# A recurrence with a mixture of experts on one core: side pieces due one block later, history ring cleared before the routing, rank products per choice

## What is computed

```python
dt = soft_clamp(softplus(xn @ Wdt.T + bdt), 0.001, 0.1, 0.5)
dA = exp(soft_clamp(dt[..., None] * A, -8.0, 8.0, 0.5));  dB = dt * (xn @ WB.T)
def step(h, inp):                      # 1024 steps, in order
    h = dAt * h + dBt * xt[..., None]
    h_norm = sqrt(sum(h * h, axis=(1, 2)))
    h = h * minimum(20.0 / (h_norm + 1e-08), 1.0)
    y = einsum('bdn,bn->bd', h, Ct) + Dp * xt
```

## Time and profile before

| | |
|---|---|
| device time, median of 3 | 1767.44 us (1767.29 to 1767.97) |
| device time of the profiled execution | 1766.3 us |
| its span, first to last instruction | 1764.2 us |
| DVE busy | 1550.5 us (88%) |
| PE busy | 1302.9 us (74%), granted clock 0.862 |
| ACT busy | 1227.6 us (70%) |
| POOL busy | 770.1 us (44%) |

### The profile page before, as it was taken

How to read it: one execution, slowest core, us unless ns; L and a number is a source line. 1 busy time by engine, 2 the same in 40 slices (tenths; PEclk the granted TensorE clock), 3 DMA queues, 4 the chain that set the end, 5 groups by cost and what they waited for, 6 DMA issues and landing times.

```text
span 1764.2 us, 33864 instructions
## 1 busy us (share of the span) xinstructions
PE 1302.9 (74%) x9352; PEld 1143.0 (65%) x9352; DVE 1550.5 (88%) x9455; ACT 1227.6 (70%) x3152; POOL 770.1 (44%) x1254
## 2 busy tenths in 40 slices
PE   5674434389879797987979797987979697835661
PEld 5553433378768686876868686876868586734551
DVE  6588888888979998997989899998989799997778
ACT  4587547388687887868687877878787777746451
POOL 3146666533434343433434343343434344468842
PEclk8577767699999898988989899998999899967885
DMA  9921111200111020111102002011101110012245
GB/s 335 340 92 49 46 43 42 96 25 24 41 55 37 25 71 24 37 59 31 31 17 91 18 26 71 27 41 34 55 24 49 40 31 19 19 34 73 75 126 195
DMA packets 95533, 113.29 MB, mean 64 GB/s; under 512 B 8432, under 2 KB 85360, under 8 KB 95344
## 3 DMA queue, kind: packets, MB, share of 16 engines
q1 hardware_dynamic: 87696, 94.13, 16.6%
q0 software_dynamic: 6144, 16.79, 3.0%
q10 hardware_dynamic: 1504, 0.22, 0.1%
HBM read 60.91 MB, written 50.20 MB: 63 GB/s over the span
## 4 chain that ended last, share of the span: by engine, by line
DVE 47%; PE 23%; ACT 9%; issue 8%; POOL 8%; DMA 3%; POOLq 0%; SPq 0%; DVEq 0%; ACTq 0%
DVE arena L756 10%; DVE arena L733 8%; DVE arena L745 7%; DVE arena L741 7%; DVE arena L727 7%; DVE arena L760 4%; PE ps L1213 4%; PE ps L1197 4%; POOL arena L536 4%; ACT arena L875 4%; PE ps L1185 4%; POOL xg L515 3%; PE ps L1160 3%; PE ps L1179 2%; DVE arena L730 2%
## 5 line engine op out<-in xcount | busy, mean ns | idle before, releaser
L536 POOL TENSOR_TENSOR arena<-arena,neghalf 128x1 f32<-128x1 f32 x1025 | 591.7, 577 | 881.1 <-DVE arena L730 812.0
L756 DVE SCALAR_TENSOR_TENSOR arena<-arena 128x128 f32<-128x128 f32 x1024 | 362.6, 354 | 53.3 <-POOL arena L536 53.1
L1185 PE MATMUL ps<-arena,pick 128*128 128x128 f32 x2048 | 306.7, 298 | 39.5 <-ACT arena L971 20.1
L1185 PEld LDWEIGHTS ps<-arena,pick 128*128 128x128 f32 x2048 | 285.1, 214 | 51.3 <-ACT arena L971 38.2
L971 ACT ACTIVATE arena<-ps,arena 128x128 f32<-128x128 f32 x1024 | 292.2, 377 | 35.1 <-PE ps L1185 34.7
L1179 PE MATMUL ps<-ident,arena 128*128 128x128 f32 x1024 | 211.8, 335 | 136.9 <-ACT arena L875 132.0
L1197 PE MATMUL ps<-arena,wf 128*128 128x256 f32 x1280 | 302.8, 387 | 8.1 <-issue 8.1
L741 DVE CUSTOM_DVE_ANT_0 arena<-arena 128x128 f32<-128x128 f32 x1024 | 294.2, 287 | 10.1 <-PE ps L1144 7.7
L1213 PE MATMUL ps<-wp,arena 128*128 128x256 f32 x1280 | 296.2, 385 | 5.4 <-ACT arena L979 5.1
L733 DVE CUSTOM_DVE_ANT_0 arena<-arena 128x128 f32<-128x128 f32 x1024 | 299.1, 292 | 0.0
L727 DVE TENSOR_TENSOR arena<-arena 128x128 f32<-128x128 f32 x1024 | 289.9, 283 | 4.5 <-POOLq L531 4.5
(11 more groups left out here) (147 smaller groups left out, 1380.3 us busy)
## 6 DMA issues: line engine op xcount, KB each, us to landing
xg<-zeros SPq DMA_DIRECT2D x10, 1024.0 KB, 9.1
xrow<-xg SPq DMA_DIRECT2D x40, 256.0 KB, 2.8
yg<-arena SPq DMA_DIRECT2D x40, 256.0 KB, 2.2
arena<-in_x SPq DMA_DIRECT2D x16, 512.0 KB, 9.3
wf<-in_c_fc SPq DMA_DIRECT2D x8, 1024.0 KB, 5.0
wp<-in_c_proj SPq DMA_DIRECT2D x8, 1024.0 KB, 5.9
arena<-dx SPq DMA_DIRECT2D x66, 64.0 KB, 2.3
ys<-arena SPq DMA_DIRECT2D x66, 64.0 KB
```

Source lines behind the costliest of these rows:

```text
L536: g.tensor_tensor(sv[:, slot, 1:2], mx, neghalf[:, 0:1], ALU.pow).then_inc(s_ready, 1)
L756: v.scalar_tensor_tensor(hr[:, slot, :], vv, sv[:, before, 1:2], ur[:, slot, :], ALU.mult, ALU.add)\
L1185: last = t.matmul(ps[2][:, j * P:(j + 1) * P], pick[:, q * QUAD + j, :], xin, start=True, stop=True)
```

## The change

Four edits. (1) The windows of all three kinds of pieces move one block (16 steps) later. (2) The routing's tiles leave `hr`'s memory: the small ones go behind the windows, into the experts' buffers, and the four large ones into `wp`. With that POOL clears `hr` and the windows without waiting for `route_ready`. (3) As `wp` is in use until then, SP loads tiles 8 to 15 (home 1) after `route_ready`. (4) The copy into `ohb` is gone. PE forms the rank products for each choice on its own, two of 256 columns as soon as the choice's one-hot array is there, and two more for the second. A new semaphore `rt_out` takes over the last use of `rt_in`.

```diff
-        at2 = [hr_at]
+        at2 = [hr_at + RING * P + BLK * NG * WIN]
...
-        ohb = lay(NE * 2 * JT).rearrange("p (e k j) -> p e k j", e=NE, k=2)
-        ohf = lay(NE * 2 * JT).rearrange("p (e k j) -> p e k j", e=NE, k=2)
...
+        ohf = wp.rearrange("p k d -> p (k d)")[:, 0:512].rearrange("p (e k j) -> p e k j", e=NE, k=2)
...
-            for table, pieces, lo_, hi_ in ((sum_at, 1, 4 * h - 9, 4 * h - 7), (input_at, 2, 4 * h - 6, 4 * h - 4), (norm_at, 1, 4 * h - 3, 4 * h - 1)):
+            for table, pieces, lo_, hi_ in ((sum_at, 1, 4 * h - 8, 4 * h - 6), (input_at, 2, 4 * h - 5, 4 * h - 3), (norm_at, 1, 4 * h - 2, 4 * h)):
...
             load_rows(0)
-            load_rows(1)
             sp.wait_ge(route_ready, 1)
-            for n in range(2, 6):
+            for n in range(1, 6):
                 load_rows(n)
...
             g.memset(sv, 1.0).then_inc(init_win, 1)
-            pool.wait_ge(route_ready, 1)
             g.memset(hr, 0.0).then_inc(h_ready, 1)
             g.memset(win, 0.0).then_inc(init_win, 1)
...
-                hop(v.tensor_tensor(ohf[:, :, k, :], iom, eix[:, k, :].unsqueeze(1).broadcast_to([P, NE, JT]), ALU.is_equal))
+                v.tensor_tensor(ohf[:, :, k, :], iom, eix[:, k, :].unsqueeze(1).broadcast_to([P, NE, JT]), ALU.is_equal).then_inc(rt_in, 1)
                 if k == 0:
+                    dve.wait_ge(rt_in, 1)
                     hop(v.scalar_tensor_tensor(lgw, ohf[:, :, 0, :], -3e38, lg, ALU.mult, ALU.add))
             v.tensor_tensor(pw[:, 0, :], top[:, 1, :], top[:, 0, :], ALU.subtract).then_inc(gap_ready, 1)
-            v.tensor_copy(ohb, ohf).then_inc(rt_in, 1)
...
-            v.tensor_copy(slot_of[:, :, :], rank).then_inc(rt_in, 1)
+            v.tensor_copy(slot_of[:, :, :], rank).then_inc(rt_out, 1)
...
-            pe.wait_ge(rt_in, 1)
-            flat = ohb.rearrange("p e k j -> p (e k j)")
-            t.matmul(ps[7][:, :], lows, flat, start=True, stop=True)
-            t.matmul(ps[6][:, :], ones[:, :], flat, start=True, stop=True).then_inc(rank_ps, 1)
+            for k in range(2):
+                pe.wait_ge(rt_in, k + 1)
+                for weights, bank in ((lows, 7), (ones[:, :], 6)):
+                    last = t.matmul(ps[bank][:, :].rearrange("p (e k j) -> p e k j", e=NE, k=2)[:, :, k, :], weights, ohf[:, :, k, :],
+                                    start=True, stop=True)
+            last.then_inc(rank_ps, 1)
...
-            waiting = [rt_in, 2]
+            waiting = [rt_out, 1]
```

More of the change, by code:

```diff
@@ L160, in build @@
         tmp = lay(NE * JT).rearrange("p (e j) -> p e j", e=NE)
-        ohb = lay(NE * 2 * JT).rearrange("p (e k j) -> p e k j", e=NE, k=2)
-        ohf = lay(NE * 2 * JT).rearrange("p (e k j) -> p e k j", e=NE, k=2)
-        tot = lay(NE * 2 * JT).rearrange("p (e k j) -> p e k j", e=NE, k=2)
-        inc = lay(NE * 2 * JT).rearrange("p (e k j) -> p e k j", e=NE, k=2)
-        keepm = lay(NE * 2 * JT).rearrange("p (e k j) -> p e k j", e=NE, k=2)
+        ohf = wp.rearrange("p k d -> p (k d)")[:, 0:512].rearrange("p (e k j) -> p e k j", e=NE, k=2)
+        tot = wp.rearrange("p k d -> p (k d)")[:, 512:1024].rearrange("p (e k j) -> p e k j", e=NE, k=2)
+        inc = wp.rearrange("p k d -> p (k d)")[:, 1024:1536].rearrange("p (e k j) -> p e k j", e=NE, k=2)
+        keepm = wp.rearrange("p k d -> p (k d)")[:, 1536:2048].rearrange("p (e k j) -> p e k j", e=NE, k=2)
         lows = lay(P)
@@ L170, in build @@
         keep = lay(2 * JT).rearrange("p (k j) -> p k j", k=2)
-        rank_i = lay(2 * JT).bitcast(i32).rearrange("p (k j) -> p k j", k=2)
-        lo_i = lay(2 * JT).bitcast(i32).rearrange("p (k j) -> p k j", k=2)
-        hi_i = lay(2 * JT).bitcast(i32).rearrange("p (k j) -> p k j", k=2)
         rowid_i = lay(2 * JT).bitcast(i32).rearrange("p (k j) -> p k j", k=2)
@@ L233, in build @@
         rt_in = sem("rt_in")
+        rt_out = sem("rt_out")
         rank_ps = sem("rank_ps")
```

## The result

The changed kernel takes 1705.61 us (median of 4 runs, 1704.60 to 1709.90), against 1767.37 us for the kernel before, run beside it. The ratio is 0.9659, with a 95% interval from 0.9638 to 0.9681: 61.8 us or 3.4% faster. The forecast was 1691, with 1681 to 1717 as the range, so the direction and the range held. The likeliest case (1682 to 1699) did not: the range held because it was drawn to take in rival (a), in which ACT and PE don't speed up, and the time is that rival's.

What follows compares the result with a forecast made beforehand. The prediction took DVE's waits for ACT's logs at the pieces as the bound: span 1764.2 - 8.7 (prologue) - 75.2 (waits) + 7.5 (coming back) = 1687.8, profiled 1689.9, median 1691 us, range 1681 to 1717.

Steps and rivals of the forecast that it cites:

- likeliest case: Whole kernel: the forecast, with nothing to 15 us of the removed waits coming back, 1682 to 1699 us; chance 0.62.
- rival (a): ACT and PE don't speed up, or slow by up to 1%: 19.5 to 30 us come back, 1703 to 1717; chance 0.27.
- What bounds the kernel, and which wait goes: DVE's waits for ACT's logs at the pieces L623 and L629, 70.1 + 5.1 = 75.2 us, go.
- What is late next: ACT and PE, slower than DVE by 2.2 us a cycle: waits at L741, step 15 of blocks 4g+3.
- plain walk: All blocks walked forward with ACT's durations, its waits taken out, and DVE's step times: 19.5 of 75.2 us come back.
- The shortening of ACT's cycle: Eight of ten blocks 4g+3 save 0 to 3 us without a waiting start; 1.5 taken, so 7.5 us come back.
- The prologue, 8.7 us: Before DVE's first L741: earlier totals 2.2, no wait for clearing 4.5, none for the output product 2.0; bounds 5 to 9.5.
- The clearing beside DVE's work: POOL's clearing beside DVE's normalization: cost taken as 0, at most 4.4 us; by the skill's rule the prologue gains 4.3.
- SP's later load: SP's load of tiles 8 to 15 behind `route_ready`: cost 0, or 2 us if PE's cover before step 16 is gone.
- (b): The whole wait reappears as one for quads, only the prologue's gain stays: 1725 to 1762 us; chance 0.04.
- (c): Later pieces come too late for their users, tightest at `squares_of`; slower than before, 1781 at 7 us a half; chance 0.03.
- (d): The wait at L623 stays, as logs end over 16 steps later: only the prologue's 1759 us; chance 0.01.

Runs made afterwards that it cites:

- the pieces' own experiment: The kernel before with only the windows of all pieces one block later: 1715.3 us, ratio 0.9710 (0.9689 to 0.9732).
- the experiment with it alone: The changed kernel with the pieces' windows as before, so only the prologue's edits: 1753.9 us, ratio 0.9943 (0.9926 to 0.9960).
- the last experiment: The changed kernel with sums and inputs one block later again, norms as in the change: 1702.3 us, ratio 0.9649 (0.9621 to 0.9677).

## Why the prediction was right, and where it was off

**What bounds the kernel, and which wait goes.** Right. The 75.2 us of the earlier trace rows went entirely, in the blocks that were named, and the pieces' own experiment has the gain on its own.

**What is late next.** Right in kind and place: L736, step 15 of blocks 4g+3, quad 0 of the next block, up to 3.8 us each. The plain walk, with ACT's durations as they were, said 19.5 us, and DVE waits 22.1 us in blocks 12 to 51.

**The shortening of ACT's cycle, which made 19.5 into 7.5.** This is the term that failed, and with it the likeliest case. I had 962.6 us for ACT and PE without ACT's waits for DVE and POOL, less 12 for faster blocks 4g+3, which is 950.6. It took 963.3 in the changed kernel, with those waits gone. In the ten blocks 4g+3 of ACT themselves, 353.5 us became 340.3. Of these 13.2 us 9.5 are the waits for POOL's coefficients in these blocks, already counted in the 15.5 of the earlier trace rows, and 3.7 are left of the 12. In the other blocks 4.4 us of what I had taken out came back.

PE's row, which I had not summed, tells why. Here is PE's window of before for the same blocks, and its waits in them, before and after:

```profile
403.60:1407.40 1003.80, 857.58 (x6183) 757.85 (x6182) 918.67 (x5800) 770.81 (x1957) 380.17 (x680) 0.93 0.13 41
```

```profile
PE ps L1179 <- ACT arena L875: 89.9, 10, 9.0
PE ps L1140 <- ACT arena L925: 30.1, 14, 4.7
```

```profile
PE ps L1176 <- ACT arena L870: 89.9, 10, 9.0
...
PE ps L1137 <- ACT arena L920: 5.4, 7, 2.9
```

The clock's gain did come on PE: its busy time fell from 857.6 to 845.0 us with as many products, at a mean granted clock of 0.95 instead of 0.93. That is 12.6 us, as large as I had it. But I had taken ACT's waits out of the cycle in full, 41.2 us, and what PE's row could give up was its own waits for the windows, 30.1 us. During ACT's waits PE was mostly at work. The longest one, at the start of block 43 before, ACT first and then PE:

```profile
1170.50 0.23 ACT L954 ACTIVATE arena<-be 128x32 f32<-128x32 f32 x1 [4.77 <-DVE arena L760]
```

```profile
1165.26 3.62 PE L1213 MATMUL ps<-wp,arena 128*128 128x256 f32 x16
1173.49 0.49 PE L1140 MATMUL ps<-arena,ident 128*128 128x128 f32 x2 [4.61 <-ACT arena L925]
```

PE works until 1168.9 and stands idle behind that, for the most part after ACT has gone on. Over all the waits of the earlier trace rows PE is busy for 30 of the 41 us, and its own waits at L1140 lie beside ACT's for only 10 us. It worked off what was queued, and that work needs its time when the wait is gone. 1003.8 - 30.1 - 12.6 = 961.1, and 963.3 was measured, with 5.4 us of such waits left and 3.2 us less of others. I had named this as the argument for rival (a) and set it aside, because PE "stood idle too": its row would have said for how long.

The rows for the clock were also badly picked. I called eight of the ten blocks 4g+3 slow and put it on the wait at their start. But block 19 began with a wait of 1.23 us and took 32.5 us (570.9 to 603.4), less than blocks 35 and 47, and block 43, behind the longest wait, took 36.0, less than block 27 with its 39.4 behind 1.6 us. Block 15 moves 74 GB/s, and blocks 35 and 47 only 21: it is one in which the expert changes. In the changed kernel, where none starts with a wait, block 15 takes 33.6 us, block 27 38.1 and block 35 32.9. The windows of PE for the last two:

```profile
745.50:783.60 38.10, 26.15 (x153) 0.82 0.23 73
942.50:975.40 32.90, 23.91 (x156) 0.90 0.07 21
```

**The prologue, 8.7 us.** 8.2 at the first L736, 6.4 at block 9 in this execution, and in the experiment with it alone 8.3 at block 52 and 10 us by the ratio (7 to 13). The parts: the totals came 1.71 us earlier (73.73 against 75.44), not 2.2. The products took what was forecast, but the one-hot array ahead of them came 0.37 us late (L683 at 71.07, L688 at 70.70 in the earlier trace rows), for which the next point has the cause. The waits for the clearing (4.52) and for the output product (2.04) went as forecast.

**The clearing beside DVE's work.** I took 0. It cost DVE 0.6 us at the last normalization: four instructions in 1.97 us, where the four of the chunk before take 1.38. The same four take 1.36 in both kernels that clear after the routing (the one before and the one with the pieces alone), and 1.95 to 2.07 in the eleven with the early clearing. It is one instruction of the four:

```profile
53.78 1.02 DVE L597 TENSOR_SCALAR arena<-arena,mv,rstd 128x256 f32<-128x256 f32 x1
```

The others take 0.40 us each. The slow one runs beside POOL's second memset (L523, 53.66 to 54.66), and starts when the long one is over. In all eleven traces one instruction that starts within 0.16 us of that memset takes 1.01 to 1.11 us and ends 0.15 us after it. About 0.35 us of it reaches the routing. The Trainium skill's rule (GPSIMD Engine Reference, section 1, Specifications) names two kinds of DVE instructions that contend with GpSimd, those with two SBUF inputs and those in a 2-port mode. L606 and L634, with two inputs, ran beside the long memset of `hr` (L522) in 1.23 and 1.10 us, as in before, where nothing runs on POOL at that time:

```profile
51.34 1.23 DVE L611 TENSOR_TENSOR wf<-arena 128x1024 f32<-128x1024 f32 x1 [1.25 <-DMA dx<-wf]
52.48 1.10 DVE L639 SCALAR_TENSOR_TENSOR arena<-arena 128x128 f32<-128x128 f32 x4
53.41 1.36 DVE L602 TENSOR_SCALAR arena<-arena,mv,rstd 128x256 f32<-128x256 f32 x4
```

The trace doesn't bear out the first kind there, so the 4.3 us worked out from it are wrong. No instruction with two inputs ran beside L523. The slowed one has one tensor input. It would fit the second kind, but no row shows in which mode it ran.

**SP's later load.** No cost was seen at step 16, as forecast.

**Rivals.** (a) is what happened, for the reason named in it. (b) is out: ACT's and PE's cycle didn't grow. (c) did not come: ACT waits nowhere at L844 or L828 for DVE in the changed kernel, and the last experiment shows where it would. (d) is out.

## What to carry to other kernels

When a wait is removed, the next bound is a row of some engine, and its floor has to be summed on that engine: its busy time plus the waits that stay. Taking the waits of a neighbour out of the neighbour's cycle claims the time in which the engine behind it was catching up. To find which of two coupled engines sets the pace, make each lighter in turn, and look at how much lighter each really got. Here 32 us less for ACT gave 4, about what executions differ, and 88 us less for PE gave all that there was. A pause that stands in the one block looked at need not be there in the others: a filling placed by block 16 was plain work in 13 of 14 places. A piece of work that isn't urgent is best due well behind its supplier, even a block too late, as long as its consumer has slack where it then waits.

## What the runs showed of the hardware

- POOL memsets beside DVE: beside the one of 128x4096 two-input operations stayed at 1.23 us (128x1024) and 1.10 us (four of 128x128), and the memset took 3.59 us instead of 3.51. A one-input 128x256 operation (L597) that started within 0.16 us of the start of the one of 128x896 took 1.01 to 1.11 us instead of 0.40, and ended 0.15 us after the memset, in eleven traces of eleven.
- Two fp32 products of 512 columns took 2.08 and 1.72 us at a granted clock of 0.50, of 256 columns 1.22 and 1.06, with an output in runs of 32 columns out of every 64: half the columns cost more than half, and the runs nothing that can be seen.
- PE's mean granted clock was 0.82 to 0.90 in stretches with the 9.0 us wait (ACT's blocks 15, 27, 35 and 47 of the changed kernel), and over blocks 12 to 51 0.95, and 0.99 once the wait was filled with 7.31 us of products, at no gain in time.
- An exponential over runs of 16 columns in steps of 64 took 1899 ns for 2048 elements a partition, over contiguous ones 1897.
